# Spreading the combine weights of a two-layer hybrid model: DMAs in place of matmuls in the wide feed-forward stages

## The reference

```python
E, K, I, SI = (16, 4, 176, 704)
routing_probs = jax.nn.softmax(x @ gate_w.T, axis=-1)
topk_w, topk_idx = jax.lax.top_k(routing_probs, K)
topk_w = topk_w / topk_w.sum(axis=-1, keepdims=True)
combine = (jax.nn.one_hot(topk_idx, E) * topk_w[..., None]).sum(1)
shared = _silu_mul(x @ shared_gate_up.T, SI) @ shared_down.T
shared = shared * jax.nn.sigmoid(x @ shared_gate_vec.T)
for each expert e:                       # h = silu(gate) * up, I = 176 channels
    acc += _silu_mul(x @ w_gu[e].T, I) @ w_d[e].T * combine[:, e][:, None]
return shared + acc
```

## Time and profile before

| | us |
|---|---|
| median of 3 runs | 4378.23 |
| the three runs | 4376.72, 4378.23, 4392.27 |
| the profiled execution, its own time | 4388.44 |
| its span, first to last instruction | 4386.7 |
| PE busy in the span | 3812.8 (87%) |
| DVE, ACT, POOL busy | 2547.1 (58%), 1716.1 (39%), 1356.8 (31%) |

### The profile page before, as it was taken

One profiled execution on the slowest core, in us unless ns is written; L12 is line 12 of the kernel. 1 busy time (PEld: TensorE's weight loads), 2 busy tenths in 40 slices (PEclk: granted clock), 3 DMA queues, 4 the chain that ended last, 5 costly groups with the idle time before them and its releaser, 6 DMA issues. The chain is left out here.

```text
span 4386.7 us, 45573 instructions
## 1 busy us (share of the span) xinstructions
PE 3812.8 (87%) x16352; PEld 2470.1 (56%) x16352; DVE 2547.1 (58%) x4291; ACT 1716.1 (39%) x2934; POOL 1356.8 (31%) x1074
## 2 busy tenths in 40 slices
PE   5879888887988886999998988999888888889999
PEld 3657644445754443555555546788744444367887
DVE  5655456664456665767676756433466776564333
ACT  2423255653235552333333323222256656532222
POOL 3224312213321104333333324444322221144442
PEclk8989989998989987999999998999989999989999
DMA  2000000001000002000010111000000000010000
GB/s 75 1 22 21 14 1 1 1 1 43 17 6 6 5 22 77 25 20 25 19 26 17 27 34 38 26 26 19 19 1 1 1 1 1 6 42 22 26 9 20
DMA packets 32909, 83.35 MB, mean 19 GB/s; under 512 B 6320, under 2 KB 7472, under 8 KB 32304
## 3 DMA queue, kind: packets, MB, share of 16 engines
q1 hardware_dynamic: 32688, 80.44, 6.1%
HBM read 59.44 MB, written 4.19 MB: 15 GB/s over the span
## 5 line engine op out<-in xcount | busy, mean ns | idle before, releaser
L1175 DVE TENSOR_REDUCE max_cols<-ps 128x1 fp32r<-128x512 f32 x1024 | 634.7, 681 | 219.6 <-PE ps L1105 218.7
L1150 ACT ACTIVATE probs<-ps 128x512 f32<-128x512 f32 x1024 | 549.9, 606 | 262.1 <-PE ps L1114 173.4
L768 POOL TENSOR_TENSOR h_lo<-h,h_hi 128x512 fp32r<-128x512 f32 x304 | 392.1, 1290 | 819.2 <-ACT h_hi L853 819.2
L932 DVE TENSOR_TENSOR gated<-silu,ps 128x512 f32<-128x512 f32 x288 | 198.1, 688 | 680.6 <-PE ps L235 656.5
L847 ACT ACTIVATE silu<-ps 128x512 f32<-128x512 f32 x304 | 181.6, 598 | 896.8 <-PE ps L235 896.7
L233 PE MATMUL ps<-xn_hi,w_hi 128*128 128x512 f32 x1216 | 483.1, 397 | 0.0
L234 PE MATMUL ps<-xn_lo,w_hi 128*128 128x512 f32 x1216 | 476.9, 392 | 0.0
L235 PE MATMUL ps<-xn_hi,w_lo 128*128 128x512 f32 x1216 | 476.3, 392 | 0.0
L338 POOL CAST o_hi<-o_scaled 128x512 fp32r<-128x512 f32 x64 | 39.0, 610 | 869.2 <-DVE o_scaled L1197 869.2
L1120 PE MATMUL ps<-probs,v_aug 128*32 128x512 f32 x2048 | 294.9, 650 | 0.5 <-ACT probs L1150 0.5
L1105 PE MATMUL ps<-k_alone,q_stack 128*128 128x512 f32 x512 | 215.4, 444 | 53.8 <-DVE max_cols L1175 24.9
(11 more groups left out here) (462 smaller groups left out, 7842.7 us busy)
## 6 DMA issues: line engine op xcount, KB each, us to landing
raw<-in_w_ffn SPq DMA_DIRECT2D x76, 448.0 KB, 3.2
raw<-raw SPq DMA_DIRECT2D x256, 64.0 KB, 2.0
composed_inputs<-in_m_latent SPq DMA_DIRECT2D x2, 2560.0 KB, 9.4
raw<-in_w_mamba SPq DMA_DIRECT2D x8, 448.0 KB, 5.8
raw<-in_w_latent SPq DMA_DIRECT2D x5, 448.0 KB, 6.3
x<-in_x SPq DMA_DIRECT2D x4, 512.0 KB, 6.7
gated_pattern<-gated SPq DMA_DIRECT2D x4, 512.0 KB, 3.4
raw<-gated_pattern SPq DMA_DIRECT2D x4, 512.0 KB, 4.4
```

The source lines that it names most:

```text
L768: nc.gpsimd.tensor_tensor(HL[:, b % 3, :], hb[:, b % 2, :], HH[:, b % 3, :].bitcast(F32), ALU.subtract).then_inc(G.sem, G.step((s, ev)))
L932: nc.vector.tensor_tensor(ga if routed(i) else hb[:, i % 2, :], sg[:, i % 2, :], bank[2 + i % 2], ALU.mult).then_inc(V.sem, V.step((s, "ga ...
L1150: nc.scalar.activation(self.PB[:, n % 8, :], self.scores(n), ACT.Exp, scale=self.scale).then_inc(A.sem, A.step((s, ("exp", n))))
L1175: nc.vector.tensor_reduce(self.MB[:, self.tile_of(g, h) % 2, q, col:col + 1], self.psum(ev), op=ALU.max, axis=AX.X, negate=True).then_inc( ...
```

## The change

In the wide stages (`j = 1`) and from the second group on, `weights(i)` issues nothing on PE. Instead the combine weights of a token block, 17 rows (16 experts and the shared gate) of 512 tokens, are copied once from the bank ROUTE to SBUF by ACT in `turned` and stored by a DMA in a DRAM tensor, `combine_rows`. For each later step three steps ahead, ACT issues after `hi` one or two DMAs that read the row of each expert the tile touches, repeated over that expert's partitions, into one of three buffers `SPREAD` (128 x 512, 256 KB). `h` then multiplies `gated` with that buffer. The DVE in `combine` makes one more small copy, the full-precision weights at columns 64 to 80 of `cw`, so that the transpose brings them to partitions 64 to 80.

The diff, whole but for its file names:

```diff
@@ -177,6 +177,10 @@
         kept, fetched = sem("gated_pattern_kept"), sem("gated_pattern_fetched")
         comp_in, comp_out_in = sem("composed_inputs_in"), sem("composed_outputs_in")
         swapped = sem("rope_halves_swapped")
+        NSPREAD = 3
+        rows_kept, spread_in = sem("combine_rows_kept"), [sem(f"combine_spread_in{i}") for i in range(NSPREAD)]
+        combine_rows = nc.dram_tensor("combine_rows", (E_[1] + 1, T), F32, kind="Internal").ap()
+        rows_stored, spreads = [0], [0] * NSPREAD
         gated_pattern = nc.dram_tensor("gated_pattern", (P, KD, T), F32, kind="Internal").ap()
         x_in, c_in, stored = [sem(f"x_in{b}") for b in range(NB)], sem("c_in"), sem("stored")
         raws, c_loads = [0], [0]
@@ -684,6 +688,9 @@
             idx = alloc("idx", [P, QT, 8], U32)
             idf = alloc("idf", [P, QT, 8])[:, :, :]
             dummy = alloc("dummy", [P, 1])[:, :]
+            if j:
+                RW = alloc("combine_whole", [P, L])[:, :]
+                SPREAD = alloc("combine_spread", [P, NSPREAD, L])[:, :, :]
             sg = alloc("silu", [P, 2, L])[:, :, :]
             ga = alloc("gated", [P, L])[:, :]
             hb = alloc("h", [P, 2, L])
@@ -735,6 +742,18 @@
             def routed(i):
                 return seq[i][0] * gt + seq[i][2] < NR
 
+            def by_matmul(i):
+                return routed(i) and (j == 0 or seq[i][0] == 0)
+
+            def by_dma(i):
+                return routed(i) and not by_matmul(i)
+
+            def experts_of(i):
+
+                r0 = (seq[i][0] * gt + seq[i][2]) * P
+                owner = [min((r0 + p) // I_[j], NE - 1) for p in range(P)]
+                return [(e, owner.index(e), owner.index(e) + owner.count(e)) for e in sorted(set(owner))]
+
             def sync(sp, s):
                 pieces = [(io[f"w_ffn{j}"][t], TW + P) for t in range(nt)]
                 send_pieces(sp, pieces, first[s], 0, ahead(s))
@@ -775,6 +794,8 @@
                     kind, b = ev
                     if ev in route_no and route_no[ev]:
                         pe.wait_ge(V.sem, V.at((s, route[route_no[ev] - 1])))
+                        if j and route[route_no[ev] - 1][0] == "turned":
+                            pe.wait_ge(A.sem, A.at((s, route[route_no[ev] - 1])))
                     if kind in ("mean", "var"):
                         if kind == "var":
                             pe.wait_ge(A.sem, A.at((s, ("squared", b))))
@@ -811,7 +832,7 @@
                     elif kind == "weights":
                         i = b
                         g, ch, t = seq[i]
-                        if routed(i):
+                        if by_matmul(i):
                             if g == 0 and t == 0:
                                 pe.wait_ge(V.sem, V.at((s, ("turned", ch))))
                             if i:
@@ -834,6 +855,14 @@
                     kind, b = ev
                     if kind in ("squared", "dev"):
                         front_act(act, s, ev, xc, sq, roots)
+                    elif kind == "turned" and j:
+                        act.wait_ge(V.sem, V.at((s, ev)))
+                        if rows_stored[0]:
+                            act.wait_ge(rows_kept, 16 * rows_stored[0])
+                        nc.scalar.activation(RW[64:64 + NE, :], ROUTE[64:64 + NE, :], ACT.Copy).then_inc(A.sem, A.step((s, ev)))
+                        act.wait_ge(A.sem, A.at((s, ev)))
+                        act.dma_start(combine_rows[0:NE, b * L:(b + 1) * L], RW[64:64 + NE, :]).then_inc(rows_kept, 16)
+                        rows_stored[0] += 1
                     elif kind == "exp":
                         act.wait_ge(V.sem, V.at((s, ("logits", b))))
                         nc.scalar.activation(pr, lg[:, :, 0:E], ACT.Exp).then_inc(A.sem, A.step((s, ev)))
@@ -851,6 +880,15 @@
                         if i >= 3:
                             act.wait_ge(PE.sem, PE.at((s, ("down", i - 3))))
                         nc.scalar.activation(HH[:, i % 3, :], hb[:, i % 2, :], ACT.Copy).then_inc(A.sem, A.step((s, ev)))
+                        n = i + NSPREAD
+                        if n < N and by_dma(n):
+                            act.wait_ge(rows_kept, 16 * rows_stored[0])
+                            ch = seq[n][1]
+                            for e, p0, p1 in experts_of(n):
+                                act.dma_start(SPREAD[p0:p1, n % NSPREAD, :], combine_rows[e:e + 1, ch * L:(ch + 1) * L].to_broadcast([p1 - p0, L])
+                                              ).then_inc(spread_in[n % NSPREAD], 16)
+                                spreads[n % NSPREAD] += 16
+                            table[(s, "spread", n)] = spreads[n % NSPREAD]
 
             def vec(dve, s):
                 def after_last():
@@ -918,7 +956,10 @@
                         nc.vector.tensor_copy(cw[:, :, 0:NE].bitcast(F32R), cwr[:, :, 0:NE]).then_inc(V.sem, V.step())
                         after_last()
                         nc.vector.tensor_tensor(cw[:, :, NE:2 * NE], cwr[:, :, 0:NE], cw[:, :, 0:NE],
-                                                ALU.subtract).then_inc(V.sem, V.step((s, ev)))
+                                                ALU.subtract).then_inc(V.sem, V.step())
+                        if j:
+                            nc.vector.tensor_copy(cw[:, :, 64:64 + NE], cwr[:, :, 0:NE]).then_inc(V.sem, V.step())
+                        V.mark((s, ev))
                     elif kind == "turned":
                         dve.wait_ge(PE.sem, PE.at((s, ev)))
                         nc.vector.tensor_copy(CT[:, b * L:(b + 1) * L], ROUTE).then_inc(V.sem, V.step((s, ev)))
@@ -931,10 +972,14 @@
                         after_last()
                         nc.vector.tensor_tensor(ga if routed(i) else hb[:, i % 2, :], sg[:, i % 2, :], bank[2 + i % 2],
                                                 ALU.mult).then_inc(V.sem, V.step((s, "gated", i)))
-                        if routed(i):
+                        if by_matmul(i):
                             after_last()
                             dve.wait_ge(PE.sem, PE.at((s, "weights", i)))
                             nc.vector.tensor_tensor(hb[:, i % 2, :], ga, WEIGHTS, ALU.mult).then_inc(V.sem, V.step())
+                        elif by_dma(i):
+                            after_last()
+                            dve.wait_ge(spread_in[i % NSPREAD], table[(s, "spread", i)])
+                            nc.vector.tensor_tensor(hb[:, i % 2, :], ga, SPREAD[:, i % NSPREAD, :], ALU.mult).then_inc(V.sem, V.step())
                         V.mark((s, ev))
                     elif kind == "added":
                         ch = seq[b][1]
```

## The result

Over 4 runs the changed kernel took 4348.9 us in the median (4342.01 to 4355.23), the kernel before 4385.25 us in its 4 (4376.72 to 4395.7): a ratio of 0.9918, interval 0.9896 to 0.9939. It is 0.8% faster. A second set of 5 runs gave 0.9918 again (0.9903 to 0.9932). The profiled execution took 4355.23 us, its span is 4353.4, against 4386.7 before.

The account below looks back on a forecast made before the run. PE was taken as the bound, busy 40 of 40 us from the wide stages' second group on. 4388.4 - 38.1 + 4.5 = 4354.8 us for the profiled execution, 4344.6 against the median; range 4332 to 4370.

Parts of the forecast that it names:

- What goes, -38.1 us: Wide stages from the second group on: 168 weights matmuls leave PE at 0.2267 us each, -38.1 us.
- What comes on the path, +4.5 us: DVE's added small copy in `combine`, before the transpose PE waits for: 8 times 0.565 us, bounds 1.6 to 13.3.
- the signs: Trace marks of a right forecast, among them PE's wait for `combine` some 2 us longer in each stage.
- Landing, ACT's issues, the row copies, 0: Wide stages: spreading transfers, their issue on ACT and ACT's copies of ROUTE all hidden, costing 0.
- `h` with a second SBUF operand: On the DVE beside POOL: `h` often 1 to 2 us, maximum near 2.5, absorbed by the margins, 0.
- The 7 us kept in the range for four late `added`: Wide groups two and three: `h` locked out by POOL's cut delays `added`, at worst 4 times 1.7 us.
- Rival A: Spreading DMAs: one repeated row is served slowly, 8.0 us per 256 KB, total about 5005 us; chance 12%.
- Rival B: Changed steps: late `h` and ACT's issues stall PE, +22 us, leaving 4367 us; chance 13%.
- Rival C: PE: more gaps lower the granted clock below 1.00; needs Rival A or Rival B first, no chance of its own.
- The sum: Whole kernel: 4354.8 us against the profiled execution, 4344.6 us against the median, 0.77% less.

Follow-up runs that it names:

- E1: Changed kernel with the 168 weights matmuls put back on PE, results unused, everything added kept; 4389.01 us, ratio 1.0012 to the kernel before.
- E2: Changed kernel without the 240 spreading DMAs, `h` multiplying by an SBUF buffer filled once; 4348.86 us, ratio 0.9911 to the kernel before.
- E3: Changed kernel whose spreading DMAs read 128 different rows of a weight tensor instead of one row repeated; 4350.77 us, ratio 0.9915 to the kernel before.
- E6: Changed kernel with two spreading buffers in place of three; 4357.91 us, ratio 0.9934 to the kernel before.
- E7: Changed kernel with every spreading DMA issued again one step later into the same buffer; 4349.76 us, ratio 0.9934 to the kernel before.
- E9: Changed kernel extended to the narrow stages from their second group on, 24 more matmuls replaced; 4358.81 us, ratio 0.9934 to the kernel before.
- E10: The changed kernel, unchanged, run and traced once more beside E9; 4348.4 us, ratio 0.9918 to the kernel before.
- E5: Changed kernel with one spreading buffer in place of three; 4407.83 us, ratio 1.0038 to the kernel before.
- E8: As E2, but `h` takes its factor from the PSUM bank of the last weights matmul; 4343.27 us, ratio 0.9895 to the kernel before.

## Why the prediction was right

Point by point, against its own steps:

- *What goes, -38.1 us.* Right, and E1 gives it by itself. From the last `weights` of the first group to the last `added`, a stage is 3163.6 - 2796.4 = 367.2 us before and 3147.4 - 2798.8 = 348.6 after, -18.6; the second stage the same, 367.2 and 348.6, and so in the trace of every kernel that has the change's steps there (E2, E3, E6, E7, E9, E10). That is -37.2 against -38.1: the 84th step has no following step, its `weights` lay beside `gated`, and its `h` is 0.2 us longer.
- *What comes on the path, +4.5 us.* The one term of the sum that was mis-sized. The copy took 191 to 193 ns all 8 times, 1.5 us in all: it never met POOL. The cast that I took for its price had met it, and took 1.66 us, once in either stage. Nor did the wait for `combine` become 2 us longer, as the signs had it: 18.5 us for 19.0 in the first stage. The first groups are as long as before at the same granted clock (E1), so the term is under 1 us and can't be told from nothing.
- *Landing, ACT's issues, the row copies, 0.* Right in the wide stages (E1, E2, E7, and no wait of PE or `h`). ACT's issues took 0.34 us in the median and not 0.59. The cover of ACT's copy is the wide block's length: E9 shows it gone.
- *`h` with a second SBUF operand.* Right that it would be longer and stall nothing, too high in the size: 0.89 us in the median and 1336 ns at most, where I had 1 to 2 us often and some 2.5 at most. The 7 us kept in the range for four late `added` did not come in the change, because the order is another than I drew: `h` meets `lo`, and the cut stands behind `h` and waits for it. In E5, where `h` is late for another reason, it does meet the cut, and there PE waits.
- *Rival A* had the right sign in the landing, 3.1 us for 2.7 (E3), and its price of 8.0 us was far off. *Rival B*: no wait of PE in either stretch. *Rival C*: clock 1.00 in both.
- *The sum.* The span fell by 33.3 us, of which -21.7 and -18.6 in the wide stages and +7 outside them (+5.5 before the first, +1.6 between), where the code is the same. The stages were to become 17 to 19 us shorter each; the 3 us beyond that in the first go with the higher clock of that one execution and not with the change. In the change's second trace it is -18.3 and -18.6, and -3 outside. What is outside scatters by more than the small terms: in the traces of the change, E1 to E8 and E10 the first wide stage begins between 2603.7 and 2616.5 us. So the median, 4348.9 us, lies 4 us above the forecast of 4344.6 though the +4.5 was not there. That the total came so close is in part luck; the gain of 37 us in the wide stages is not. (The low end of the forecast's own range adds up to 4333 and not 4335.)

Not settled: where the 5 us of E1's ratio lie, if they are there at all, and why the same code takes a granted clock of 0.87 in most executions of the first group and 0.89 or 0.90 in some.

## What to carry to other kernels

Price a matmul by the distance between starts in a stretch where PE never waits, and multiply only by those that lie in such a stretch: the same edit was worth 0.227 us apiece there, nothing in a group whose pace another engine set, and it lost where its preparation lay on the path. Work moved from the bound engine to DMAs was free here as long as the loop from buffer free to data landed and used, divided by the buffers, stayed below the step in its longest form: with one buffer it was 3.97 us against 4.08 in the good case and 5.6 when `h` met POOL. Before you explain a difference of a few us by the edit, compare stage by stage, in several traces, and look at the granted clock of the stage. When an operand moves from PSUM to SBUF on the DVE, look at what POOL does at that moment, and at what is queued behind.

## What the hardware showed that was not expected

- A DMA written behind an activation on ACT is issued before that activation runs (3091.71 against 3092.11 in E5; in the change by 0.1 to 0.4 us, mostly 0.4, when a `silu` is running ahead of it). As these rows read, the issue waits for the semaphores that the instructions ahead wait for, not for their execution. ACT's issue took 308/344/617 ns for these DMAs.
- One 2 KB row read by DMA into 128 partitions lands in 3.1 us, 128 different rows of another tensor in 2.7; with twice the spreading traffic, 151 GB/s in all, the one row takes 4.0 us.
- The DVE's two-operand read of SBUF and POOL delay each other: `h` 687 to 893 ns in the median, POOL's cast 930 to 1415 ns in every one of 14. An `h` that meets a POOL instruction ends 0.5 to 0.6 us after it, whether that is `lo` in the change or the longer cut in E5.
